# A cross-attention scan and an eight-expert layer on one core: the first conv, the hand-over to the first expert, and the order of the first copies

## The chip, the core and the metric

The kernel runs on one core of a Trainium2 chip. The metric is the device time of one execution in microseconds (us), lower is better. Engines are named as in the profile: PE is TensorE (PEld its weight loads), DVE is VectorE, ACT is ScalarE, POOL is GpSimd, SP is SyncE, which here only issues DMAs.

## The reference, cut to what matters

```python
# 1: selective scan over ctx (4 batches x 256 tokens), gated by the layer norm of x
x_in = einsum('ed,bld->bel', in_proj_w, ctx)              # 128 -> 256 channels
xc   = depthwise causal conv over time, 4 taps            # conv_w [256, 4]
u    = silu(xc + conv_b)
x_dbl = einsum('ke,bel->bkl', x_proj_w, u)                # dt_lo 8, B 16, C 16
delta = softplus(dt_proj_w @ dt_lo + dt_proj_b)
state = state * exp(delta * A) + (delta * u) * B          # 16 states per channel, 256 steps
y     = sum_n(state * C) + D * u
x     = x + (y * silu(layernorm(x)))^T

# 2: mixture of experts: 8 experts, the best 2 per token, at most 320 tokens each
probs = softmax(layernorm(x) @ Wg); gate, idx = top_k(probs, 2)
h     = relu(rows @ w1[e])                                # 256 -> 1024
out   = h @ w2[e]                                         # 1024 -> 256
x     = x + sum over the two experts of gate * out
```

## The kernel before

The work has two halves. In the first, four batches `b` of 256 tokens go through the scan; channels lie on partitions in two chunks `c`. A batch has eight steps `p` of two states each (`g = 8 b + p`, 32 steps). ACT writes the decays to PSUM, POOL the driving products `dbu`, DVE runs the scan and the product with C, PE adds the products into `y`. Everything is ordered by hand: each engine has one instruction stream and waits on named semaphores.

**The first conv.** For batches 1 to 3 the conv runs on PE: eight f32 matmuls of `ctxs`, shifted by a tap each, with folded weights `cwb` = taps times `in_proj_w` (`conv`, L783). POOL makes all of `cwb` in one multiply (L337) when the taps, copied to every partition by a DMA that is the fourth on ACT's queue (L489), are there. Batch 0 does not wait for this: PE projects `ctxs` with the bare weights (L905), and DVE applies the taps in eight operations from PSUM (L1206, L1209) into `conv0`. ACT makes `u` of both chunks (L614), PE multiplies by `wdt` (`first_dt`, L776), and ACT begins the softplus at L521. PE meanwhile goes on with `b_cast(0)`, `project`, `b_cast(1)` (L802, L756, L802), whose last result ACT copies at L538 before it makes the first decays. `keep_clock(n)` is n matmuls of ones by ones (L753) whose result nobody reads.

**The end of batch 3.** After the last step, DVE gates and adds x, and takes the layer norm's statistics; POOL raises the variance to the power -1/2 (L436); DVE makes `nmx`, minus mean over deviation (L1422), after it has chosen the two experts (`choose`); ACT makes the normalised rows (L690) and splits them into a rounded part and a rest (L693). `add_zeros(4)` adds four matmuls of zeros to `y` (L848) after steps 2, 3, 4 and 5 of this batch.

**Experts.** Each matmul of the experts is done in three: rounded part by rounded part, and each rounded part by the other's rest (`split_mm`, L1035 to L1037). So ACT makes `w1hi`, `w2hi`, `xthi`, `hthi`, and DVE or POOL the rests `w1lo`, `w2lo`, `xtlo`, `htlo`, weights by quarters. `h` has eight parts `f`; four PSUM banks hold them, so part f waits for the `htlo` of part f-4. Expert 0 gets the last batch's rows by a matmul with 0/1 columns `takes` (L1136), the others from DRAM: POOL sends every token's row by indirect DMAs into `expert_rows` (`send`, L401), SP reads an expert's rows (`rows_in`), PE turns them (`turn_rows`). For the first expert PE runs the first chunk of w1 for f = 0 to 3 (L1073, L1078), then the second chunk in the same way, and only its last four matmuls complete the four parts. `w2` of expert 0 is loaded during batch 3; ACT splits it between the relus (L708), POOL makes all four rests (L445). POOL then fetches the result rows so far (`fetch`, L455), DVE adds the expert's gated rows in the next expert (L1462, between the `htlo` of f = 1 and f = 2), and POOL sends them back (L464).

## Time and profile before

| | |
|---|---|
| median of 3 runs | 291.98 us (291.63 to 294.25) |
| the profiled execution, its own time | 291.21 us |
| its span, first to last instruction | 289.2 us |
| busy: PE, DVE, POOL, ACT | 240.7, 223.6, 222.9, 174.9 us |
| mean granted TensorE clock | 0.934 |

The scan takes the span up to about 147 us, the experts the rest. Busy shares are means over both. The granted clock is printed as a share of full speed, 1.00 for 2.4 GHz and 0.50 for 1.2 GHz; a window's value is a mean. A f32 matmul shows as two instructions.

### The profile page before, as it was taken

The page shows a single profiled execution, that of the slowest core. Times are in us where ns is not written, and L with a number is a line of the kernel's source. Part 1 is how long each engine was busy: PE and PEld are TensorE (multiplying, and loading weights), DVE is VectorE, ACT ScalarE, POOL GpSimd, SP SyncE. Part 2 cuts the span into 40 slices and gives each one's busy share as a digit, 9 for nine tenths or more (in the row PEclk, how much of TensorE's full clock was granted, in tenths as well). Part 3 has the DMA queues.
Part 4 walks back from the last instruction along what each step waited for, and adds up shares of the span by engine and source line. Part 5 has one row for each costly group of instructions (what it writes and reads, how often), then busy time and mean ns, then how long its engine had stood idle before and what let it go on. Part 6 is the DMA issues. An engine that isn't in the chain of part 4 may idle for free.

```text
span 289.2 us, 5036 instructions
## 1 busy us (share of the span) xinstructions
PE 240.7 (83%) x1568; PEld 220.2 (76%) x1568; DVE 223.6 (77%) x371; ACT 174.9 (60%) x384; POOL 222.9 (77%) x177
## 2 busy tenths in 40 slices
PE   8957695595957396668799899999999999999990
PEld 7745484475845285557798798999999999999980
DVE  2799999799899999999966766858585757575710
ACT  2889757948996776669017736475655647374500
POOL 1779779869996999999732958878787878787761
PEclk9999979888999957589799999999999999999997
DMA  6679630063003804042041566355564655655110
GB/s 160 229 201 339 209 134 0 2 201 129 0 3 97 268 0 183 2 154 101 21 137 25 200 216 217 113 210 194 170 196 187 190 214 178 226 179 180 38 59 23
DMA packets 15073, 40.38 MB, mean 140 GB/s; under 512 B 2922, under 2 KB 9900, under 8 KB 12112
## 3 DMA queue, kind: packets, MB, share of 16 engines
q1 hardware_dynamic: 11792, 33.15, 34.1%
q0 software_dynamic: 2816, 6.32, 6.4%
q10 hardware_dynamic: 448, 0.70, 1.0%
q8 instruction: 8, 0.13, 0.2%
q14 instruction: 9, 0.07, 0.1%
HBM read 32.72 MB, written 8.49 MB: 143 GB/s over the span
## 4 chain that ended last, share of the span: by engine, by line
PE 35%; POOL 6%; DVE 4%; issue 4%; DMA 3%; ACT 1%; POOLq 0%; DVEq 0%; ACTq 0%; SPq 0%
PE ps L1035 9%; PE ps L1037 9%; PE ps L1036 9%; POOL w2lo L445 3%; DVE h L1261 2%; DMA w2raw<-in_w 2%; PE ps L1044 1%; PE ps L839 1%; POOL out L464 1%; DVE hc L1273 1%; PE ps L1051 1%; DMA so_far<-out,dst 1%; PE ps L1073 1%; POOL so_far L455 1%; PE ps L753 1%
## 5 line engine op out<-in xcount | busy, mean ns | idle before, releaser
L356 POOL TENSOR_TENSOR dbu<-du,bsb 128x1024 f32<-128x1024 f32 x31 | 73.7, 2396 | 1.8 <-DMA bsb<-b_rows 0.8
L552 ACT ACTIVATE ps<-delta,anegs 128x255 f32<-128x255 f32 x128 | 53.0, 461 | 12.6 <-DVE h L1254 9.3
L1451 DVE SCALAR_TENSOR_TENSOR htlo<-ps,hthi 128x320 fp32r<-128x320 f32 x64 | 30.8, 488 | 33.6 <-ACT hthi L717 33.6
L817 PE MATMUL ps<-stack,sels 64*128 64x256 f32 x64 | 17.0, 352 | 36.8 <-DVE hc L1273 33.6
L817 PEld LDWEIGHTS ps<-stack,sels 64*128 64x128 f32 x64 | 10.8, 210 | 44.4 <-issue 44.0
L445 POOL TENSOR_TENSOR w2lo<-w2raw,w2hi 128x512 fp32r<-128x512 f32 x30 | 39.1, 1330 | 6.3 <-ACT w2hi L708 6.2
L455 POOL DMA_INDIRECT so_far<-out,dst x24 | 33.3, 1386 | 11.6 <-issue 4.7
L839 PE MATMUL ps<-cst,hc 128*128 128x128 f32 x256 | 41.7, 317 | 0.0
L1254 DVE TENSOR_TENSOR_SCAN h<-ps,dbu 128x1024 f32<-128x1024 f32 x18 | 41.1, 2283 | 0.5 <-issue 0.3
L1035 PE MATMUL ps<-xthi,w1hi 128*128 (+1 forms) x120 | 37.8, 315 | 1.2 <-DVE htlo L1451 1.2
L717 ACT ACTIVATE hthi<-ps 128x320 fp32r<-128x320 f32 x64 | 27.7, 438 | 17.1 <-PE ps L1037 15.3
L1273 DVE TENSOR_TENSOR hc<-h,ps 128x1024 f32<-128x1024 f32 x31 | 37.1, 1197 | 0.8 <-DVE h L1254 0.8
L1037 PE MATMUL ps<-xthi,w1lo 128*128 (+1 forms) x120 | 37.1, 309 | 0.0
L1036 PE MATMUL ps<-xtlo,w1hi 128*128 (+1 forms) x120 | 37.1, 309 | 0.0
L839 PEld LDWEIGHTS ps<-cst,hc 128*128 128x128 f32 x256 | 33.8, 163 | 3.9 <-issue 1.1
L1035 PE MATMUL ps<-hthi,w2hi 128*128 128x320 f32 x112 | 35.3, 315 | 0.8 <-issue 0.8
L1037 PE MATMUL ps<-hthi,w2lo 128*128 128x320 f32 x112 | 34.6, 309 | 0.0
L1036 PE MATMUL ps<-htlo,w2hi 128*128 128x320 f32 x112 | 34.6, 309 | 0.0
L1261 DVE TENSOR_TENSOR_SCAN h<-ps,dbu 128x512 f32<-128x512 f32 x28 | 32.7, 1210 | 1.8 <-ACT ps L552 1.8
L464 POOL DMA_INDIRECT out<-eo,dst x24 | 23.7, 988 | 6.9 <-issue 6.9
L401 POOL DMA_INDIRECT expert_rows<-xrow,sloti x16 | 16.2, 1014 | 11.5 <-ACT xrow L701 6.6
L1035 PEld LDWEIGHTS ps<-xthi,w1hi 128*128 128x128 f32 x120 | 22.5, 188 | 1.7 <-issue 0.9
(181 smaller groups left out, 533.1 us busy)
## 6 DMA issues: line engine op xcount, KB each, us to landing
w1raw<-in_w SPq DMA_DIRECT2D x8, 1024.0 KB, 5.2
w2raw<-in_w SPq DMA_DIRECT2D x8, 1024.0 KB, 4.8
bsb<-b_rows SPq DMA_DIRECT2D x7, 1024.0 KB, 7.2
expert_rows<-fill SPq DMA_DIRECT2D x1, 2580.0 KB, 15.6
xe<-expert_rows SPq DMA_DIRECT2D x8, 258.0 KB, 5.4
out<-x SPq DMA_DIRECT2D x4, 256.0 KB, 5.3
xnat<-in_x SPq DMA_DIRECT2D x1, 768.0 KB, 7.2
xe<-expert_rows SPq DMA_DIRECT2D x8, 64.5 KB, 5.5
```

The lines of the kernel that those rows point to most:

```text
L356: nc.gpsimd.tensor_tensor(dbu[j % DRING][:], du[:, :, None, cols(b)].to_broadcast([P, EC, 2, L]), bsb[b % 2][:, None, 2 * p:2 * p + 2, :]. ...
L445: nc.gpsimd.tensor_tensor(w2lo[:, fs, :], w2raw[:, fs, :], w2hi[:, fs, :].bitcast(F32), ALU.subtract).then_inc(s["w2lo_done"], 1)
L455: nc.gpsimd.indirect_dma_start(so_far[0:EROWS[t], t, :], None, out, bass.IndirectOffsetOnAxis(ap=dst[0:EROWS[t], e * ET + t, :], axis=0), ...
L552: ins = nc.scalar.activation(decays(g % SLOTS_DA)[:, c, i * L + 1:(i + 1) * L], delta[:, c, b * L + 1:(b + 1) * L], ACT.Exp, scale=anegs[: ...
L839: ins = nc.tensor.matmul(y[:, t, c * P:(c + 1) * P], hc[g % SUMS][:, c, i, t * P:(t + 1) * P], ident, start=False, stop=(g % PAIRS == PAIR ...
L1035: nc.tensor.matmul(out_, hi_a, hi_b, start=start, stop=False)
L1036: nc.tensor.matmul(out_, hi_a, lo_b, start=False, stop=False)
L1037: return nc.tensor.matmul(out_, lo_a, hi_b, start=False, stop=stop)
L1254: nc.vector.tensor_tensor_scan(h[g % HRING][:].rearrange("p c n t -> p (c n t)"), decays(g % SLOTS_DA).rearrange("p c t -> p (c t)"), dbu[ ...
L1261: nc.vector.tensor_tensor_scan(h[g % HRING][:, c].rearrange("p n t -> p (n t)"), decays(g % SLOTS_DA)[:, c, :], dbu[g % DRING][:, c].rearr ...
L1273: nc.vector.tensor_tensor(hc[g % SUMS][:].rearrange("p c n t -> p c (n t)"), h[g % HRING][:].rearrange("p c n t -> p c (n t)"), ps[:, c_ba ...
L1451: nc.vector.scalar_tensor_tensor(out=htlo[:, f, :], in0=ps[:, f % 4, 0:CAP], scalar=0.0, in1=hthi[:, f, :].bitcast(F32), op0=ALU.max, op1= ...
```

## The change

- **Start.** The taps' copy becomes ACT's first DMA, `in_proj_w` SP's first, ctx of batch 0 second, the small dt weights third; the first rows of x move behind `sel`. DVE makes the folded weights, one chunk at a time (two operations on 512 elements); POOL no longer does. PE runs batch 0's conv with them in two sets of four matmuls (`first_conv`) around the small `dts` product, after ten `keep_clock` matmuls in place of six; two more come behind, where six were. DVE's eight tap operations and PE's two projections are gone. The negation of `anegs` goes from DVE to POOL; on ACT the exp that feeds it and the copy of `sels` go behind the first softplus pieces.
- **End of batch 3.** `add_zeros` after steps 2 to 5 is 4, 4, 6, 2 in place of 4, 4, 4, 4. `nmx` is made by POOL from a negated mean that DVE makes before `choose`. Two `keep_clock` matmuls ahead of the last `logits` are gone.
- **First expert.** ACT splits expert 0's w2 after steps 5 and 6 of batch 3. Its first two rests are made by DVE between the first `htlo`, the last two by POOL. The second chunk of w1 runs part by part, so that part 0 is complete after three matmuls. POOL sends all first copies of the last batch's rows before the second ones; ACT writes the gates before both second copies. `turn_rows(1)` runs after f = 5 of the output in place of f = 4.

PE at the start of the program, before:

```order
L753 MATMUL ps<-onesf 128x128 x6
L905 MATMUL ps<-ctxs,inps 128x256 x2
L753 MATMUL ps<-onesf 128x128 x2
L910 MATMUL ps<-dts 128x256 x2
L753 MATMUL ps<-onesf 128x128 x6
L776 MATMUL ps<-u,wdt 128x256 x4
```

and in the changed kernel:

```order
L771 MATMUL ps<-onesf 128x128 x10
L922 MATMUL ps<-ctxs,cwb 128x256
L922 MATMUL ps<-ctxs,cwb 128x255
L922 MATMUL ps<-ctxs,cwb 128x254
L922 MATMUL ps<-ctxs,cwb 128x253
L931 MATMUL ps<-dts 128x256 x2
L922 MATMUL ps<-ctxs,cwb 128x256
L922 MATMUL ps<-ctxs,cwb 128x255
L922 MATMUL ps<-ctxs,cwb 128x254
L922 MATMUL ps<-ctxs,cwb 128x253
L771 MATMUL ps<-onesf 128x128 x2
L794 MATMUL ps<-u,wdt 128x256 x4
```

Two projections have become eight conv matmuls, and the second four stand behind the `dts` product and ahead of `first_dt`.

DVE at the start of the first expert (`xtlo` and `htlo` are rests of its rows and of h), before:

```order
L1504 TENSOR_TENSOR xtlo<-ps,xthi 128x320 x2
L1370 TENSOR_TENSOR w1lo<-w1raw,w1hi 128x2x256 x2
L1451 SCALAR_TENSOR_TENSOR htlo<-ps,hthi 128x320 x8
L1370 TENSOR_TENSOR w1lo<-w1raw,w1hi 128x2x256 x2
L1438 COPY gates<-xe 128x2
```

and in the changed kernel:

```order
L1520 TENSOR_TENSOR xtlo<-ps,xthi 128x320 x2
L1384 TENSOR_TENSOR w1lo<-w1raw,w1hi 128x2x256 x2
L1470 SCALAR_TENSOR_TENSOR htlo<-ps,hthi 128x320
L1445 TENSOR_TENSOR w2lo<-w2raw,w2hi 128x512
L1470 SCALAR_TENSOR_TENSOR htlo<-ps,hthi 128x320
L1445 TENSOR_TENSOR w2lo<-w2raw,w2hi 128x512
L1470 SCALAR_TENSOR_TENSOR htlo<-ps,hthi 128x320 x6
```

Two rests of w2 stand between the first three `htlo`.

ACT from the last batch's weights (`etop`) to the first relu (`xrow<-etop` are the gates, `xrow<-x` the second copies of the rows), before:

```order
L587 ACTIVATE etop<-top,ntop,rx 128x8 x2
L735 ACTIVATE xthi<-ps 128x320 x2
L701 ACTIVATE xrow<-x,nmx,rx 128x256
L596 ACTIVATE xrow<-etop,rsum 128x2 x2
L701 ACTIVATE xrow<-x,nmx,rx 128x256
L717 ACTIVATE hthi<-ps 128x320
L708 ACTIVATE w2hi<-w2raw 128x512
```

and in the changed kernel:

```order
L602 ACTIVATE etop<-top,ntop,rx 128x8 x2
L753 ACTIVATE xthi<-ps 128x320 x2
L611 ACTIVATE xrow<-etop,rsum 128x2 x2
L725 ACTIVATE xrow<-x,nmx,rx 128x256 x2
L735 ACTIVATE hthi<-ps 128x320 x8
L620 ACTIVATE w1hi<-w1raw 128x2x256 x2
```

The gates stand ahead of both second copies, and no split of w2 stands between the eight relus any more.

The diff, cut:

```diff
+            sp.dma_start(inps[:], inproj_t).then_inc(s["inp_in"], 16)
             sp.dma_start(ctxs[:, cols(0)], ctx_t[:, cols(0)]).then_inc(s["ctx_in0"], 16)
+            sp.dma_start(dts[:], dt_small).then_inc(s["dts_in"], 16)
             sp.dma_start(xps[:], xproj_t).then_inc(s["xps_in"], 16)
+            sp.dma_start(brow[0:XPC, 0:BC], sel).then_inc(s["sel_in"], 16)
             sp.dma_start(xnat[:, tiles_of(0), :], x[:, tiles_of(0), :]).then_inc(s["x_in0"], 16)
-            sp.dma_start(brow[0:XPC, 0:BC], sel).then_inc(s["sel_in"], 16)
...
-            pool.wait_ge(s["inp_in"], 16)
-            pool.wait_ge(s["cw_in"], 16)
-            nc.gpsimd.tensor_tensor(cwb[:], cwb[:], inps[:, None, :].to_broadcast([P, TAPS, DI]), ALU.mult
-                                    ).then_inc(s["cw_done"], 1)
+            z_rstd(1, tiles_of(0))
+            pool.wait_ge(s["a_exp"], 1)
+            nc.gpsimd.tensor_scalar(anegs[:], anegs[:], -1.0, None, ALU.mult).then_inc(s["a_neg"], 1)
             pool.wait_ge(s["small_in"], 32)
...
+            pool.wait_ge(s["ln_rstd"], B)
+            pool.wait_ge(s["mean_neg"], 1)
+            nc.gpsimd.tensor_tensor(nmx[:, tiles_of(B - 1)], pmx[:], rx[:, tiles_of(B - 1)], ALU.mult
+                                    ).then_inc(s["ln_scale"], 1)
             pool.wait_ge(s["xe_in"], 32)
-            for j in tiles_range(B - 1):
-                send(j)
+            pool.wait_ge(s["gates_done"], B)
+            pool.wait_ge(s["slots_done"], B)
+            for k in range(TOPK):
+                for t in range(BT):
+                    j = (B - 1) * BT + t
+                    if k:
+                        pool.wait_ge(s["xn_done"], j + 1)
+                    else:
+                        pool.wait_ge(s["row_done"], t + 1)
+                    nc.gpsimd.indirect_dma_start(
+                        xe_dram, bass.IndirectOffsetOnAxis(ap=sloti[:, j, k:k + 1], axis=0),
+                        xrow[:, j, k, :], None, bounds_check=SLOTS - 1, oob_is_err=False
+                    ).then_inc(s["scattered1"], 16)
...
+                if e == 0:
+                    pool.wait_ge(s["w2lo_done"], WP // 2)
+                for m in range(0 if e else WP // 2, WP // 2 if e == NE - 1 else WP):
...
-            act.dma_start(inps[:], inproj_t).then_inc(s["inp_in"], 16)
+            act.dma_start(cwb[:], conv_w[None, :, :].to_broadcast([P, TAPS, DI])).then_inc(s["cw_in"], 16)
             act.dma_start(ch[:], chan).then_inc(s["ch_in"], 16)
-            act.dma_start(dts[:], dt_small).then_inc(s["dts_in"], 16)
-            act.dma_start(cwb[:], conv_w[None, :, :].to_broadcast([P, TAPS, DI])).then_inc(s["cw_in"], 16)
             nc.scalar.preload_act_table(ACT.Silu)
...
-                act.wait_ge(s["cv_done"], c + 1)
-                nc.scalar.activation(u[:, c, cols(0)], conv0[:, c, :], ACT.Silu, bias=ch[:, c, CB:CB + 1]
+                act.wait_ge(s["conv0_psum"], c + 1)
+                nc.scalar.activation(u[:, c, cols(0)], ps[:, (CBANK, BBANK)[c], 0:L], ACT.Silu, bias=ch[:, c, CB:CB + 1]
                                      ).then_inc(s["u_done"], 1)
             nc.scalar.preload_act_table_set(EXP_SET)
+            decay_exps(0, V0BANK)
             nc.scalar.activation(anegs[:], ch[:, :, ALOG:ALOG + DS], ACT.Exp).then_inc(s["a_exp"], 1)
             act.wait_ge(s["sel_in"], 16)
             nc.scalar.activation(sels[:], brow[0:XPC, 0:BC], ACT.Copy).then_inc(s["sel_done"], 1)
-            decay_exps(0, V0BANK)
             logs(0)
...
+                if b == B - 1 and p in (5, 6):
+                    for m in range(WP // 2):
+                        split_w2(0, m + (WP // 2 if p == 6 else 0))
...
-            second_row(T // P - BT)
             weigh(B - 1)
-            second_row(T // P - 1)
+            for j in tiles_range(B - 1):
+                second_row(j)
...
+            def first_conv(c):
+                pe.wait_ge(s["cw_done"], c + 1)
+                for k in range(TAPS):
+                    ins = nc.tensor.matmul(ps[:, (CBANK, BBANK)[c], k:L], cwb[:, TAPS - 1 - k, c * P:(c + 1) * P],
+                                           ctxs[:, 0:L - k], start=(k == 0), stop=(k == TAPS - 1))
+                ins.then_inc(s["conv0_psum"], 1)
+
+            keep_clock(10, V0BANK)
             pe.wait_ge(s["ctx_in0"], 16)
-            for c, bank in ((0, WBANK), (1, CBANK)):
-                nc.tensor.matmul(ps[:, bank, 0:L], inps[:, c * P:(c + 1) * P], ctxs[:, cols(0)],
-                                 start=True, stop=True).then_inc(s["xe0_psum"], 1)
-            keep_clock(2, BBANK)
+            first_conv(0)
             pe.wait_ge(s["dts_in"], 16)
             for k in range(EC):
                 ins = nc.tensor.matmul(ps[:, YBANK, k * DI:(k + 1) * DI], dts[:, DI + k * P:DI + (k + 1) * P],
                                        dts[:, 0:DI], start=(k == 0), stop=True, skip_group_check=True)
             ins.then_inc(s["wdt_psum"], 1)
-            keep_clock(6, BBANK)
+            first_conv(1)
+            keep_clock(2, V0BANK)
...
-                    add_zeros(4)
+                    add_zeros((4, 4, 6, 2)[p - 2])
...
-            keep_clock(2, DABANK + 1)
...
-                    for c in range(KC):
+                    for c in range(KC - 1):
                         pe.wait_ge(s["xthi_done"], c + 1)
                         for f in range(4):
                             if c == 0 and f % FP == 0:
...
                         pe.wait_ge(s["xtlo_done"], c + 1)
                         for f in range(4):
                             fs = slice(f * P, (f + 1) * P)
-                            ins = nc.tensor.matmul(ps[:, f, 0:CAP], w1hi[:, c, fs], xtlo[:, c, slots],
-                                                   start=False, stop=(c == KC - 1))
-                            if c == KC - 1:
-                                ins.then_inc(s["h_psum"], 1)
+                            nc.tensor.matmul(ps[:, f, 0:CAP], w1hi[:, c, fs], xtlo[:, c, slots],
+                                             start=False, stop=(c == KC - 1))
+                    pe.wait_ge(s["xthi_done"], KC)
+                    pe.wait_ge(s["xtlo_done"], KC)
+                    for f in range(4):
+                        hidden_part(f, KC - 1).then_inc(s["h_psum"], 1)
...
-                        if first and f == 5:
+                        if first and f == 6:
...
+            dve.wait_ge(s["inp_in"], 16)
+            dve.wait_ge(s["cw_in"], 16)
+            for c in range(EC):
+                cs = slice(c * P, (c + 1) * P)
+                nc.vector.tensor_tensor(cwb[:, :, cs], cwb[:, :, cs], inps[:, None, cs].to_broadcast([P, TAPS, P]),
+                                        ALU.mult).then_inc(s["cw_done"], 1)
             dve.wait_ge(s["ch_in"], 16)
-            dve.wait_ge(s["xe0_psum"], EC)
...
+            nc.vector.tensor_scalar(pmx[:], mvx[:, tiles_of(last), 0], -1.0, None, ALU.mult).then_inc(s["mean_neg"], 1)
             choose(last)
-            dve.wait_ge(s["ln_rstd"], B)
-            nc.vector.scalar_tensor_tensor(out=nmx[:, tiles_of(last)], in0=mvx[:, tiles_of(last), 0], scalar=-1.0,
-                                           in1=rx[:, tiles_of(last)], op0=ALU.mult, op1=ALU.mult
-                                           ).then_inc(s["ln_scale"], 1)
             find_key(last)
             place(last)
             sum_weights(last)
...
+                    if first and f < WP // 2:
+                        low_w2(0, f)
```

## Rows read from the trace of the kernel before

**Rows 1.** The page: the span, and two groups of its part 5.
```profile
span 289.2 us, 5036 instructions
...
L1035 PE MATMUL ps<-xthi,w1hi 128*128 (+1 forms) x120 | 37.8, 315 | 1.2 <-DVE htlo L1451 1.2
...
L1035 PE MATMUL ps<-hthi,w2hi 128*128 128x320 f32 x112 | 35.3, 315 | 0.8 <-issue 0.8
```

**Rows 2.** Timeline, 0 to 32 us: start, duration, engine, line, operation, tiles, [idle before].
```profile
0.73 0.41 ACTq L486 DMA_DIRECT2D inps<-in_inproj_t  x1
...
6.92 1.60 PE L753 MATMUL ps<-onesf 128*128 128x128 f32 x12
...
8.79 2.35 POOL L337 TENSOR_TENSOR cwb<-cwb,inps 128x1024 f32<-128x1024 f32 x1 [7.39 <-DMA cwb<-in_conv_w]
...
8.92 1.97 PE L776 MATMUL ps<-u,wdt 128*128 128x256 f32 x8 [0.40 <-ACT u L614]
...
11.19 0.81 ACT L521 ACTIVATE w1raw<-ps,ch 128x256 f32<-128x256 f32 x2
...
13.04 0.78 DVE L1224 TENSOR_TENSOR w1raw<-w1raw 128x512 f32<-128x512 f32 x1
...
15.38 1.88 PE L783 MATMUL ps<-ctxs,cwb 128*128 128x256 f32 x8
...
15.58 0.60 ACT L538 ACTIVATE bsb<-ps 128x512 f32<-128x512 f32 x1 [1.23 <-PE ps L802]
```

**Rows 3.** DMA issues by line: KB each, median us from issue to landing.
```profile
w2raw<-in_w SPq DMA_DIRECT2D x8, 1024.0 KB, 4.8
...
cwb<-in_conv_w ACTq DMA_DIRECT2D x1, 512.0 KB, 6.4
bsb<-b_rows SPq DMA_DIRECT2D x1, 512.0 KB, 4.8
...
inps<-in_inproj_t ACTq DMA_DIRECT2D x1, 128.0 KB, 2.9
```

**Rows 4.** The chain that ended last, in order of time: start, duration, what.
```profile
143.17 1.71 PE ps L848 x8
...
157.09 1.17 PE ps L1073 x8
...
175.03 2.40 DMA so_far<-out,dst
```

**Rows 5.** Windows: busy us of PE, PEld, DVE, ACT, POOL (instructions), granted clock, DMA share, GB/s.
```profile
141.80:145.40 3.60, 3.60 (x21) 3.60 (x20) 3.60 (x5) 0.00 (x0) 2.66 (x3) 0.55 0.20 73
```

**Rows 6.** Timeline, 148 to 152 us, the end of the last batch.
```profile
148.31 0.60 ACT L562 ACTIVATE xnt<-ps 128x512 f32<-128x512 f32 x1 [6.96 <-PE ps L855]
...
149.65 0.72 POOL L436 TENSOR_TENSOR rx<-vx,nhalf 128x2 f32<-128x2 f32 x1 [2.69 <-DVE vx L1418]
...
151.17 0.15 DVE L1422 SCALAR_TENSOR_TENSOR nmx<-mvx,rx 128x2 f32<-128x2 f32 x1
...
151.36 0.60 ACT L690 ACTIVATE xrow<-x,nmx,rx 128x256 f32<-128x256 f32 x1 [2.45 <-DVE nmx L1422]
```

**Rows 7.** Timeline, 157 to 159 us, the first expert.
```profile
157.01 1.04 POOL L401 DMA_INDIRECT expert_rows<-xrow,sloti  x1 [6.65 <-ACT xrow L701]
...
158.78 0.62 ACT L708 ACTIVATE w2hi<-w2raw 128x512 fp32r<-128x512 f32 x1
...
159.55 0.39 PE L1035 MATMUL ps<-xthi,w1hi 128*128 128x320 f32 x1 [0.70 <-DVE htlo L1451]
```

**Rows 8.** Timeline of TensorE, 162 to 182 us.
```profile
164.09 0.38 PE L1035 MATMUL ps<-hthi,w2hi 128*128 128x320 f32 x1 [0.78 <-issue]
...
178.50 0.42 PE L1035 MATMUL ps<-xthi,w1hi 128*128 x1 [0.52 <-DVE htlo L1451]
```

**Rows 9.** Timeline of GpSimd, 160 to 180 us.
```profile
162.72 5.93 POOL L445 TENSOR_TENSOR w2lo<-w2raw,w2hi 128x512 fp32r<-128x512 f32 x4
172.11 1.30 POOL L455 DMA_INDIRECT so_far<-out,dst  x1 [3.46 <-DVE dst L1439]
```

52 lines of the change are left out of this document (18 added, 34 removed).

## The prediction

> **What bounds the kernel now.** I read the page first, then the waits of TensorE, then the start and the hand-over in the timeline. From the first expert on, TensorE is the bound: the 232 groups of three matmuls of the experts have only 1.2 us of idle time ahead of them in w1 and 0.8 us in w2 [rows 1]. All of it lies at three places in the first two experts: 0.70 us at 159.55, 0.78 us at 164.09, 0.52 us at 178.50 [rows 7, 8]. So behind 180 us nothing is to be won, and what is won ahead of it comes out at the end in full. In the scan the steps of DVE, ACT and POOL follow each other closely, and I take it that a shift of the first decays comes out in full too. The change touches the start, the end of batch 3, and those three places.
>
> **The start.** Call L the time at which the taps have landed. Now they land 6.4 us after an issue that is the fourth on its queue, and POOL, which waits for them and nothing else, begins at 8.79 us [rows 2, 3]. Nobody is in a hurry for them. In the changed kernel everything waits for them:
> - DVE folds the first chunk: one operation of two SBUF inputs on 512 elements takes 0.78 us [rows 2], so with the wait PE can begin at L + 0.9.
> - PE then does, without a gap, eight rows of conv, four of `dts`, eight of conv, four of `keep_clock` (two matmuls), eight of `first_dt`. Eight conv rows take 1.88 us [rows 2]. The last one's drain, some 0.16, is in that; it is the difference between the 0.31 mean of an expert's matmul [rows 1] and 0.147 of spacing (1.17 over 8 [rows 4]). So eight are 1.72, and the 28 rows of 256 columns 6.0. The four of `keep_clock` take 0.5 (1.60 over 12 [rows 2]). `first_dt` is complete at L + 0.9 + 6.0 + 0.5 + 0.2 = L + 7.6.
> - Now it is complete at 8.92 + 1.97 = 10.9 [rows 2]. PE goes on from there to `b_cast(1)`, for which ACT waits 1.23 us before the copy at 15.58 [rows 2]; the first decays follow it. So this path shifts by L + 7.6 - 10.9 = L - 3.3. The other path, ACT's softplus, starts at 11.19 [rows 2] and shifts by 0.3 less; moving `anegs` and `sels` behind it helps only there. I take L - 3.3.
>
> What is L? The issue is at 0.73, like that of `inps` now [rows 2]. From rows: 128 KB on that queue land in 2.9 us, 1024 KB from DRAM in 4.8; in between by bytes, 512 KB are 3.7, and L is 4.4. The other end is the copy most like it, also 512 KB, also one source row to all partitions, which takes 4.8 [rows 3]: L is 5.5. Some 340 KB of SP's copies go out beside it. With nothing big ahead I take the lower end and a little for company, **L = 4.6, the start 1.3 us later**; the ends are 0.9 (L = 4.2) and 2.2. It would be free only at L = 3.3, quicker than the 128 KB landed. POOL loses a multiply of 2.35 us and DVE its eight tap operations, but nobody waits for either behind this. The copies of x and the constants, moved one or two issues back, have waits only behind 11 us; nothing for them.
>
> The Trainium skill ("DMA: Bandwidth & Descriptors", "Anatomy of one DMA") gives a copy some 2.0 us fixed plus its bytes at 436 GB/s, which is 3.2 us for the taps, an L of 3.9 and a start only 0.6 us later. The trace's 4.8 us for 512 KB speaks against it, its 4.8 for 1024 KB nearly for it (4.4).
>
> **The end of batch 3.** Around 142 to 145 us the granted clock is 0.55 on average, which is 1.2 GHz for most of it [rows 5], and the four `add_zeros` of step 5 then stand in the chain with 1.71 us [rows 4], ahead of the last two steps' products. Two less save 0.86 there, but they would run into the half-speed stretch 0.6 us deeper (a row takes 1.71 / 8 = 0.21 there, half of that at full speed), and the very last products wait for DVE. I take **0.3 us earlier**; 0 if the drop of the clock moves along, 0.8 if the two more zeros at step 4 keep it away. The splits of w2, four of 0.62, fall into ACT's idle 6.96 us ahead of 148.31 [rows 6, 7], at no cost; they would cost 2.5 if that idle were not there.
>
> `nmx` now comes from DVE at 151.17, behind `choose`, and ACT's rows follow at 151.36 [rows 6]. On POOL it follows the power, which begins at 149.65 and takes 0.72 [rows 6], at about 150.45, and takes some 0.2, so it ends by 150.75. ACT's chain of rows, roundings and weights behind it is busy without a gap until `xthi`, so it moves by **0.6 us**, if PE keeps up: the two `keep_clock` fewer give `logits` 0.3, and DVE has 0.15 less ahead of `takes`. The lower end is 0.3, where `takes` decides.
>
> **The first expert.** In issue times the three gaps are larger than shown by the drain of 0.16: 0.9, 0.9 and 0.7 us. Taken with PE's first matmul of the expert as the zero: the first goes, since part 0 of h is complete after 15 matmuls and not 21, 6 x 0.147 = 0.9 earlier. The two rests of w2 that DVE now makes between the `htlo` (0.7 each by the 0.78 above) leave parts 5 and 6 late by some 0.1 each. The second goes: PE waited there for POOL's first `w2lo`, begun at 162.72 [rows 8, 9], and DVE has it by 160. The output then begins at 155.1 (where the expert's first matmul stands now: 157.09 [rows 4], behind 12 of 0.147, less 0.2) + 48 x 0.147 + 0.2 = 162.3, and the last two quarters are needed 24 matmuls later, from 165.8. POOL starts its sends when the gates are there; now it starts at 157.01 [rows 7], and with the gates one second copy earlier (0.6 [rows 6]) at about 156.5. From 157.01 to 162.72 its four sends and the memset of `so_far` take 5.7 [rows 7, 9], so it comes to w2 at 162.2, and two quarters of 5.93 / 4 = 1.5 end at 165.2; no wait. That makes 1.6 up to the second expert. But the third gap is not of w2. There DVE's `htlo` of part 2 stands behind the gated rows of the first expert, and these behind the last of POOL's three fetches (175.03 plus 2.40 [rows 4]), begun at 172.11 behind the slot numbers [rows 9]. These hang on `xthi` of expert 1, thus on `turn_rows(1)`, thus on the rows' landing and PE's place: f = 6 is reached at 162.3 + 36 x 0.147 = 167.6, against 164.09 + 30 x 0.147 = 168.5 for f = 5 now. So the fetches come only 1.1 earlier, not 1.6, and the third gap grows by the rest. **Middle: 1.1 us earlier**; ends 0.7 (rows land late) and 1.9 (fetches keep pace).
>
> **Sum.** 1.3 - 0.3 - 0.6 - 1.1 = -0.7 us. The profiled execution took 291.21, so 290.5; the median is 291.98, so 291.3. The profiled one is a little below the three runs shown. I take the middle, **290.9 us**. My own range for this case is 289.9 to 292.0.
>
> **Rivals.**
> - *The taps land early* (L = 3.9, which is also the result of the Trainium skill's rule above; or the shift is swallowed in batch 0, where POOL and DVE have slack I did not see). Start +0.5 or less: 290.1 down to 289.5. For it: no copy of weight is ahead. Against: 4.8 us for its likeness. 0.17.
> - *The hand-over gives all of it*: the fetches follow PE (1.9) and the clock does not drop (0.8). 1.3 - 0.8 - 0.6 - 1.9 = -2.0: 289.6. For it: POOL has nothing else between 165 and its fetches. Against: the order xthi, numbers, fetch. 0.15.
> - *The taps come late, and it is slower than before*: all 16 DMA engines' time goes to SP's copies issued in the same microseconds, as now, when they take 6.4 us. The start loses L - 3.3, the rest gives 2.0, so from L = 5.3 on it is slower. With 6.4 us, L is 7.1 and the time 290.9 + 2.5 = 293.4; at 4.8 us, the likeness, 291.8. 0.13.
> - *A half-speed stretch moves into 145 to 156 us*, since PE does less there (two `keep_clock` and two zeros fewer): 3.4 us at half speed cost 1.7. 292.6. 0.07.
> - *It does not do what it says*: if POOL's last two quarters came behind 165.8, PE would wait as now; then the second gap stays, 291.8. In the forecast's range, with no chance of its own.
>
> **How the numbers follow.** Forecast 0.48, rivals 0.17, 0.15, 0.13, 0.07. The range leaves out the far halves of the early and full cases and the end of the late one: 289.1 to 292.9. A measurement of this kernel can tell about 1% from no change. 1% under 291.98 is 289.06, which needs the early taps and the full hand-over together: 0.09. 1% over is 294.9, taps at 8.6 or a longer clock drop: 0.04. Within: 0.87.
>
> **What will show it.** The taps' issue to landing (3.9 forecast); the end of `first_dt` (12.2); the first decays 1.3 later than now. The power and `nmx` next to each other on POOL at 150 to 151 plus the shift. PE without idle at the first relu and the first `hthi` by `w2hi`, with a gap of more than 0.5 left in expert 1 at part 6, its releaser `htlo`, behind DVE's wait for `so_far`. What would make it wrong: a start that is no later, for then my L or my path from `first_dt` to the decays is wrong; or a gap at w2's third quarter.

## The result and the profile of the changed kernel

The changed kernel takes 293.72 us (median of 20 runs, 291.76 to 298.44), the kernel before, on the same chip, 291.73 us (20 runs, 290.84 to 294.25). The ratio is 1.0045 (95% interval 1.0024 to 1.0066), that is 1.3 us slower. The ratios here and below leave disturbed runs out, two of the 20 of the changed kernel and three of the six of rest_numbers_first among them, so that 1.3 us is less than the 2.0 between the medians. The forecast was 290.9 us and faster by 0.7; the profiled executions, 293.71 against 291.21, are 2.5 apart on the other side.

The page of the changed kernel, against [rows 1]:

```profile
span 291.9 us, 5038 instructions
...
L1055 PE MATMUL ps<-xthi,w1hi 128*128 (+1 forms) x124 | 39.3, 317 | 2.1 <-DVE htlo L1470 1.8
...
L1055 PE MATMUL ps<-hthi,w2hi 128*128 128x320 f32 x112 | 35.2, 314 | 0.0
```

The span grew by 2.7 us. The idle time in w2 is gone as forecast, but w1 has 2.1 us of it where it had 1.2, and 1.8 wait for `htlo`. Now the start, against [rows 2], in the timeline of the changed kernel:

```profile
0.99 4.64 PE L771 MATMUL ps<-onesf 128*128 128x128 f32 x20 [0.99 <-POOL onesf L318]
...
4.92 1.29 DVE L1226 TENSOR_TENSOR cwb<-cwb,inps 128x512 f32<-128x512 f32 x2 [3.66 <-DMA cwb<-in_conv_w]
...
5.73 1.96 PEld L922 LDWEIGHTS ps<-ctxs,cwb 128*128 128x128 f32 x8 [0.40 <-DMA ctxs<-in_ctx_t]
5.76 2.33 PE L922 MATMUL ps<-ctxs,cwb 128*128 128x256 f32 x8
...
8.01 1.13 PE L931 MATMUL ps<-dts 8*128 8x256 f32 x4
...
9.07 1.98 PE L922 MATMUL ps<-ctxs,cwb 128*128 128x256 f32 x8
...
10.89 0.61 PE L771 MATMUL ps<-onesf 128*128 128x128 f32 x4
...
11.34 1.89 PE L794 MATMUL ps<-u,wdt 128*128 128x256 f32 x8
...
18.42 3.25 ACT L567 ACTIVATE ps<-delta,anegs 128x255 f32<-128x255 f32 x8
```

`first_dt` ends at 13.23, before at 10.89: 2.34 us later. The first decays begin at 18.42, before at 16.08 (the first row of the next fence): 2.34 too. The DMA issues, against [rows 3], show when the data came:

```profile
cwb<-in_conv_w ACTq DMA_DIRECT2D x1, 512.0 KB, 4.1
...
inps<-in_inproj_t SPq DMA_DIRECT2D x1, 128.0 KB, 3.5
ctxs<-in_ctx_t SPq DMA_DIRECT2D x1, 128.0 KB, 4.2
```

The taps need 4.1 us from issue to landing in place of 6.4. The 128 KB of ctx beside them, issued at 1.18, need 4.2. The row of the weight loads puts their wait of 0.40 us down to ctx, but ctx was there at 1.18 + 4.2 = 5.4. The first chunk's fold, 0.69 us from 4.92, ended at 5.61 and came last.

For the stages behind, four rows of the timeline of the kernel before that the groups ahead of the prediction do not have: the first decays, the last gate product, the first matmul of the first expert, and the third expert's w1 load.

```profile
16.08 1.66 ACT L552 ACTIVATE ps<-delta,anegs 128x255 f32<-128x255 f32 x4
...
146.87 0.69 DVE L1288 TENSOR_TENSOR zst<-ps,zst 128x512 f32<-128x512 f32 x1 [1.45 <-PE ps L839]
...
155.09 0.39 PE L1073 MATMUL ps<-xthi,w1hi 128*128 128x320 f32 x1
...
176.25 0.34 SPq L285 DMA_DIRECT2D w1raw<-in_w  x1
```

The end of batch 3 in the changed kernel, against [rows 6]:

```profile
149.66 0.69 DVE L1302 TENSOR_TENSOR zst<-ps,zst 128x512 f32<-128x512 f32 x1 [0.94 <-PE ps L857]
...
152.44 0.72 POOL L436 TENSOR_TENSOR rx<-vx,nhalf 128x2 f32<-128x2 f32 x1 [2.16 <-DVE vx L1432]
...
153.24 0.20 POOL L440 TENSOR_TENSOR nmx<-pmx,rx 128x2 f32<-128x2 f32 x1
...
153.47 0.60 ACT L714 ACTIVATE xrow<-x,nmx,rx 128x256 f32<-128x256 f32 x1 [1.77 <-POOL nmx L440]
...
154.97 0.85 PE L1035 MATMUL ps<-cst,xe 128*128 128x128 f32 x6 [0.31 <-DMA xe<-expert_rows]
...
157.42 0.39 PE L1093 MATMUL ps<-xthi,w1hi 128*128 128x320 f32 x1
```

`nmx` stands behind the power as forecast. ACT's first row begins 3.81 us behind the gate product, before 4.49 (151.36 less 146.87): 0.68 won. But the first matmul of the expert wins only 0.46 (7.76 behind the gate product, before 8.22), since TensorE now waits for the rows of expert 0 from DRAM. And the first expert, against [rows 7 to 9]:

```profile
158.16 1.28 DVE L1384 TENSOR_TENSOR w1lo<-w1raw,w1hi 128x512 fp32r<-128x512 f32 x2
158.86 1.51 POOL L452 DMA_INDIRECT expert_rows<-xrow,sloti  x1 [5.43 <-ACT xrow L611]
...
160.67 0.97 POOL L452 DMA_INDIRECT expert_rows<-xrow,sloti  x1 [0.30 <-issue]
160.78 0.68 DVE L1445 TENSOR_TENSOR w2lo<-w2raw,w2hi 128x512 fp32r<-128x512 f32 x1
...
161.78 0.68 DVE L1445 TENSOR_TENSOR w2lo<-w2raw,w2hi 128x512 fp32r<-128x512 f32 x1
161.95 1.36 POOL L452 DMA_INDIRECT expert_rows<-xrow,sloti  x1 [0.30 <-issue]
...
173.13 0.41 PE L1055 MATMUL ps<-xthi,w1hi 128*128 x1 [0.29 <-ACT w1hi L620]
...
173.80 1.30 POOL L470 DMA_INDIRECT so_far<-out,dst  x1 [5.39 <-DVE dst L1458]
...
176.72 0.95 POOL L470 DMA_INDIRECT so_far<-out,dst  x1 [0.31 <-issue]
...
177.61 0.35 SPq L287 DMA_DIRECT2D w1raw<-in_w  x1
...
180.23 0.48 DVE L1481 SCALAR_TENSOR_TENSOR eo<-ps,gates,so_far 64x256 f32<-64x256 f32 x1 [1.35 <-DMA so_far<-out,dst]
...
181.16 0.41 PE L1055 MATMUL ps<-xthi,w1hi 128*128 x1 [1.82 <-DVE htlo L1470]
```

The first two gaps are gone, and the third is 1.82 us where it was 0.52. It stands behind the last `eo`, which stands behind the third fetch. That one was issued 1.69 us later than before (176.72 against 175.03 [rows 4]) but is waited for until 180.23; in the kernel before the same `eo` began at 177.57. A gap of 0.29 us is new: at 173.13 the second expert's first matmul waits for ACT's `w1hi`, which stands behind `xthi`.

Step by step, in the profiled executions:

| step | forecast | measured | from |
|---|---|---|---|
| first decays | +1.3 | +2.34 | 18.42 against 16.08 |
| the scan, to the last gate product | 0 | +0.45 | 149.66 against 146.87, less 2.34 |
| end of batch 3 | -0.9 | -0.46 | 7.76 against 8.22 |
| first expert to behind the third gap | -1.1 | +0.33 | 181.16 against 178.50, less 2.33 |
| sum | -0.7 | +2.66 | |

### The profile page after: what moved, and what is told of

It reads as the page before. It is cut to its first block, busy times and chain, and to the rows that moved or that the text cites. A ratio compares the mean times of both kernels' runs of the same rounds, so it can differ in the third digit from the quotient of the medians.

```text
span 291.9 us, 5038 instructions
## 1 busy us (share of the span) xinstructions
PE 252.0 (86%) x1572; PEld 228.0 (78%) x1572; DVE 222.1 (76%) x366; ACT 175.4 (60%) x384; POOL 220.0 (75%) x176
## 4 chain that ended last, share of the span: by engine, by line
PE 40%; DVE 7%; issue 6%; POOL 4%; DMA 4%; ACT 1%; POOLq 0%; SPq 0%; DVEq 0%; ACTq 0%
PE ps L1055 11%; PE ps L1057 10%; PE ps L1056 10%; DVE hc L1287 2%; PE ps L857 2%; DVE h L1268 2%; PE ps L1064 2%; DVE h L1275 1%; DMA so_far<-out,dst 1%; POOL out L479 1%; PE ps L1071 1%; POOL so_far L470 1%; PE ps L835 1%; DMA xe<-expert_rows 1%; DMA expert_rows<-xrow,sloti 1%
## 5 line engine op out<-in xcount | busy, mean ns | idle before, releaser
L356 POOL TENSOR_TENSOR dbu<-du,bsb 128x1024 f32<-128x1024 f32 x31 | 72.7, 2364 | 1.4 <-DMA bsb<-b_rows 1.1
L857 PE MATMUL ps<-cst,hc 128*128 128x128 f32 x256 | 44.9, 332 | 1.0 <-DVE hc L1287 1.0
L835 PE MATMUL ps<-stack,sels 64*128 64x256 f32 x64 | 18.6, 380 | 27.2 <-DVE hc L1287 24.2
L1055 PE MATMUL ps<-xthi,w1hi 128*128 (+1 forms) x124 | 39.3, 317 | 2.1 <-DVE htlo L1470 1.8
L460 POOL TENSOR_TENSOR w2lo<-w2raw,w2hi 128x512 fp32r<-128x512 f32 x28 | 36.2, 1320 | 6.4 <-ACT w2hi L627 6.2
L857 PEld LDWEIGHTS ps<-cst,hc 128*128 128x128 f32 x256 | 36.3, 171 | 5.5 <-issue 2.2
L835 PEld LDWEIGHTS ps<-stack,sels 64*128 64x128 f32 x64 | 11.8, 230 | 36.0 <-issue 36.0
L1057 PE MATMUL ps<-xthi,w1lo 128*128 (+1 forms) x124 | 38.3, 309 | 0.0
L1056 PE MATMUL ps<-xtlo,w1hi 128*128 (+1 forms) x124 | 38.3, 309 | 0.0
L1056 PEld LDWEIGHTS ps<-xtlo,w1hi 128*128 128x128 f32 x124 | 23.3, 188 | 0.0
```

Of the source, the lines that this page charges most:

```text
L356: nc.gpsimd.tensor_tensor(dbu[j % DRING][:], du[:, :, None, cols(b)].to_broadcast([P, EC, 2, L]), bsb[b % 2][:, None, 2 * p:2 * p + 2, :]. ...
L460: nc.gpsimd.tensor_tensor(w2lo[:, fs, :], w2raw[:, fs, :], w2hi[:, fs, :].bitcast(F32), ALU.subtract).then_inc(s["w2lo_done"], 1)
L835: ins = nc.tensor.matmul(ps[:, c_bank(g), i * L:(i + 1) * L], sels[:, n:n + 1].to_broadcast([XPC, P]), stack[:, cols(b)], start=(i == 0), ...
L857: ins = nc.tensor.matmul(y[:, t, c * P:(c + 1) * P], hc[g % SUMS][:, c, i, t * P:(t + 1) * P], ident, start=False, stop=(g % PAIRS == PAIR ...
L1055: nc.tensor.matmul(out_, hi_a, hi_b, start=start, stop=False)
L1056: nc.tensor.matmul(out_, hi_a, lo_b, start=False, stop=False)
```

## The experiments

Two theories stood at first. *The start* (theory A): the later start is the loss, and the rest of the change is worth about nothing. *The hand-over* (theory B): the start costs what was forecast, and the loss lies in the hand-over, where the third gap eats more than the other two gave. Eleven kernels ran in three groups of four, four and three, each against the kernel before on the same chip; its medians there were 293.3, 292.7 and 293.2 us. The traces show one execution of each. In the tables, "distance" is from the last gate product to the expert's first matmul.

**start_only.** The kernel before with the diff's first part: the DMAs' order, the folded weights on DVE, `first_conv`, ten and two `keep_clock`.

```diff
 (kernel before)
+            keep_clock(10, V0BANK)
...
+            first_conv(0)
...
+            first_conv(1)
+            keep_clock(2, V0BANK)
```

> The kernel before with the start of the change alone (order of the first copies, folded weights by DVE, first conv on TensorE, anegs on GpSimd). Theory A, the start is where the time is lost: the first decays stand at 18.4 us as in the changed kernel (16.1 before), and it is 2.0 to 2.8 us slower than before. Rival B, the loss is made later, by the expert part or by half-speed stretches that only the two halves together cause: 0.5 to 1.3 us slower at most, though the decays stand late.

Measured: 295.52 us (294.56 to 297.99), ratio 1.011 (1.0041 to 1.0178). The timeline of this kernel:

```profile
5.39 1.29 DVE L1204 TENSOR_TENSOR cwb<-cwb,inps 128x512 f32<-128x512 f32 x2 [4.13 <-DMA cwb<-in_conv_w]
...
11.44 1.89 PE L773 MATMUL ps<-u,wdt 128*128 128x256 f32 x8
...
18.52 3.25 ACT L549 ACTIVATE ps<-delta,anegs 128x255 f32<-128x255 f32 x8
```

The decays come 2.44 us later than before, and all three gaps of the kernel before are there (0.70, 0.79, 0.94). So the start alone makes it slower, by 3.2 us with an interval of 1.2 to 5.2; the 2.4 that the decays show lies in it. The taps landed half a microsecond later than in the changed kernel (the fold at 5.39 against 4.92), and `first_dt` ended only 0.1 later. TensorE waited 0.61 us ahead of the conv, and its first eight rows then took 1.89 us (6.23 to 8.12), where they take 2.25 in the changed kernel.

**rest_only.** The changed kernel with the start of before.

```diff
 (changed kernel)
-            keep_clock(10, V0BANK)
+            keep_clock(6, V0BANK)
...
-            first_conv(0)
+            for c, bank in ((0, WBANK), (1, CBANK)):
+                nc.tensor.matmul(ps[:, bank, 0:L], inps[:, c * P:(c + 1) * P], ctxs[:, cols(0)],
+                                 start=True, stop=True).then_inc(s["xe0_psum"], 1)
...
-            first_conv(1)
-            keep_clock(2, V0BANK)
+            keep_clock(6, BBANK)
```

> The kernel before with everything but the start: the end of batch 3 and the first expert as in the changed kernel. Theory A: the end of batch 3 gives some 0.5 us, the second expert begins another 1.0 to 1.5 us earlier, and the third gap of TensorE (0.52 before, 1.82 in the changed kernel) takes most of it back, so it is 0.2 to 0.8 us faster. My prediction's terms would make it 2.0 us faster. Rival B: as slow as before or slower.

Measured: 292.62 us, ratio 0.9992 (0.9951 to 1.0033). So the hand-over is worth nothing that shows, where 2.0 us were forecast. Together with start_only this bears out theory A: the start is the loss, and the rest gives next to nothing. (The two do not add up to the 1.3 us of the changed kernel, but the interval of start_only reaches down to 1.2.) Two things in its trace say where the gain went. Its third gap is as long as that of the changed kernel; and a half-speed stretch lies at the end of batch 3, where the windows give a granted clock of 0.65:

```profile
152.00:156.00 4.00, 4.00 (x26) 3.94 (x26) 2.85 (x14) 2.65 (x10) 0.00 (x0) 0.65 0.20 68
...
180.57 0.41 PE L1055 MATMUL ps<-xthi,w1hi 128*128 x1 [1.87 <-DVE htlo L1478]
```

The distance is 8.87 us there, more than the 8.22 of before.

**hand_only.** The first expert's part alone: `nmx` by DVE, four zeros at each step and the two `keep_clock` before `logits` as before.

```diff
 (rest_only)
-                    add_zeros((4, 4, 6, 2)[p - 2])
+                    add_zeros(4)
...
+            keep_clock(2, DABANK + 1)
             logits(B - 1)
```

> The kernel before with the first expert's edits alone (w2 split early, two of its rests on DVE, second chunk part by part, first copies sent first, the turn of the next rows one part later). Theory A: first two gaps of TensorE gone, the third 1.5 or more: within 0.4 us of before. If the turn one part later and the slower sends are what makes the third gap, it shows here too, without the end of batch 3.

Measured: 293.69 us, ratio 1.0024 (0.9986 to 1.0061). The distance is 8.22, as before, and no half-speed stretch lies behind 145 us. The third gap is 1.36 us, a little under the 1.5 expected.

**rest_numbers_first.** While expert 0 ends, DVE copies the second expert's slot numbers, makes the rests of its rows, and only then copies expert 0's numbers. Here expert 0's numbers go ahead of the rests. POOL's three fetches wait for both sets of numbers.

```diff
 (rest_only)
-                    rows_lo(e + 1)
                     if first:
                         metas(0, True)
+                    rows_lo(e + 1)
```

> As rest_only, but DVE copies the first expert's slot numbers ahead of the rest of the second expert's rows, so that they no longer wait for ScalarE's xthi, and GpSimd can fetch the result rows some 1 to 1.9 us earlier. Theory A (the fetches are what holds the second expert): the third gap shrinks to 0.5 us or less and it is 1.0 to 1.5 us faster than rest_only. Rival: the gap is set by how long the fetches take to land, not by when they start; then it gains under 0.4 us.

Measured: 291.87 us (288.38 to 293.31), ratio 0.9875 (0.9796 to 0.9954). The ratio goes by three runs, 288.38, 288.46 and 290.78 us; the trace is of another, of 293.26. In it the third gap is gone. Expert 0's numbers need nothing of the second expert's `xthi`; they waited for it only because DVE's `xtlo` stood ahead of them. They still stand behind the second expert's own numbers, which wait for its rows from DRAM. The half-speed stretch was there again (distance 8.83).

**start_dts_first.** To see whether `dts`, which hangs on no tap, can use the wait for the taps.

```diff
 (start_only)
-            first_conv(0)
             pe.wait_ge(s["dts_in"], 16)
...
+            first_conv(0)
             first_conv(1)
-            keep_clock(2, V0BANK)
```

> As start_only, but TensorE does the small dts product ahead of the first conv, while it waits for the taps, and the two keep_clock matmuls behind the second conv are left out: 4 rows of 256 and 4 of 128 columns less between the taps and first_dt. Theory A (the start is a sum: landing of the taps and of ctx, the fold, then every row that TensorE does): first_dt ends and the first decays stand 0.9 to 1.3 us earlier than in start_only (18.5), so at 17.2 to 17.6. Rival (the two copies land late and the rest is hidden): less than 0.4 us earlier.

Measured: 294.57 us (292.33 to 296.41), ratio 1.0055 (1.0008 to 1.0101). Timeline of one execution, of 296.10 us, and the window of the conv:

```profile
5.84 2.07 PE L908 MATMUL ps<-dts 8*128 8x256 f32 x4 [0.21 <-DMA dts<-in_dt_small]
7.84 6.42 PE L901 MATMUL ps<-ctxs,cwb 128*128 128x256 f32 x16
14.10 1.89 PE L773 MATMUL ps<-u,wdt 128*128 128x256 f32 x8
```

```profile
7.90:13.60 5.70, 5.70 (x15) 4.62 (x15) 1.00 (x4) 1.07 (x2) 1.40 (x4) 1.00 0.61 238
```

The decays begin at 21.18 in this execution, 2.7 us later than in start_only, where 0.9 to 1.3 earlier was expected. No data is missing. The conv rows come 0.43 us apart up to 13.1, the last ones and `first_dt` 0.215: half the pace, then the full pace. The column says 1.00 all the same. But the trace's records of the granted clock begin only at 13.38, with 1.00; where there is no record, the column prints 1.00 too. So the pace of the rows is what can be read there, and it is that of 1.2 GHz.

The start of every kernel here shows the same. In the changed kernel the rows of the ten `keep_clock` from 0.99 stand 0.213 us apart, those of the two at 10.89 only 0.11, and its first record of the clock is at 6.51. In start_only it is at 6.10, in the kernel before at 5.08. In after_numbers_first, whose start is word for word that of the changed kernel, it is at 10.20, and its decays begin at 20.54, not 18.42. So a late rise of the clock comes without thin rows first as well, and the order of `dts` is not shown to be its cause. Nor is the move shown to be bad: the runs of this kernel spread over 4 us, the traced one is among the slowest, and the ratio is lower than that of start_only, with intervals that overlap.

**rest_w1_waits.** The load of the third expert's w1 waits until the last of the three fetches of `so_far` has landed (they count from 0).

```diff
 (rest_only)
                     sp.wait_ge(s["h_psum"], FC * (e - 1) + W1_LATER)
+                    if e == 2:
+                        sp.wait_ge(s["so_far_in2"], 16)
```

> As rest_only, but SyncE issues the third expert's w1 load only when the last of the three fetches of result rows has landed. Theory (a TensorE that is earlier releases that load earlier, and its packets meet those of the third fetch): the third fetch lands 2.4 us after its issue in place of 3.4, and the third gap of TensorE is 1.0 us, not 1.87. Rival (the fetch is slow for a reason of its own): gap 1.7 or more, as before.

Measured: one run, 290.68 us. The timeline:

```profile
176.47 0.34 SPq L286 DMA_DIRECT2D w1raw<-in_w  x1
176.53 0.48 DVE L1491 SCALAR_TENSOR_TENSOR eo<-ps,gates,so_far 64x256 f32<-64x256 f32 x1 [0.46 <-DMA so_far<-out,dst]
177.46 0.41 PE L1057 MATMUL ps<-xthi,w1hi 128*128 x1 [0.90 <-DVE htlo L1480]
```

The last `eo` waits 0.46 us in place of 1.36, and the third gap is 0.90 in place of 1.87. So in this one execution half of that gap is gone with the load held back; that the load held the fetch up fits this. Without `keep_clock` before `logits` there was no half-speed stretch here, and the distance was 7.73.

**rest_pool_rests** and **rest_all_clock.** POOL makes expert 0's first two rests of w2 in the scan, in place of DVE in the expert, with the numbers first; the second kernel also has the `keep_clock` and zeros of before.

```diff
 (rest_numbers_first)
+            for m in range(WP // 2):
+                fs = slice(m * FP, (m + 1) * FP)
+                pool.wait_ge(s["w2hi_done"], m + 1)
+                nc.gpsimd.tensor_tensor(w2lo[:, fs, :], w2raw[:, fs, :], w2hi[:, fs, :].bitcast(F32),
+                                        ALU.subtract).then_inc(s["w2lo_done"], 1)
             pool.wait_ge(s["ln_eps"], B)
...
-                    if first and f < WP // 2:
-                        low_w2(0, f)
```

> As rest_numbers_first, but the first two rests of w2 are made by GpSimd in its idle time ahead of the last power, not by VectorE between the htlo. Theory (VectorE's operations with two SBUF inputs slow the indirect sends): the third send takes 0.97 us, not 1.36, the last one ends 0.4 us earlier after the expert's start, and the wait for the rows at turn_rows(1), 0.62, falls to 0.2. The power may start up to 0.3 us later. Time within 0.5 us of rest_numbers_first.

> As rest_pool_rests, with the two keep_clock matmuls ahead of the last logits back and four add_zeros after each of the steps 2 to 5. Theory (these matmuls of no use are what keeps the hand-over at full speed): no half-speed stretch between 145 and 160 us, and 1.0 to 1.5% faster than before, the best version so far. Rival (the stretches fall where they fall, by the phase of each run): a stretch at 151 to 157 us here too, and no difference to rest_pool_rests.

Measured: 292.28 us, ratio 0.998 (0.994 to 1.0019), and 292.08 us, ratio 0.9976 (0.9937 to 1.0015). Both times missed what was expected of them. The third gap is gone in both, but the distance is 10.4 and 9.8 us. The timeline of rest_all_clock shows why:

```profile
148.21 2.52 POOL L439 TENSOR_TENSOR w2lo<-w2raw,w2hi 128x512 fp32r<-128x512 f32 x2
148.32 2.97 DVE L1442 TENSOR_TENSOR x<-zst,xnat 128x512 f32<-128x512 f32 x1
...
161.91 0.98 POOL L458 DMA_INDIRECT expert_rows<-xrow,sloti  x1 [0.31 <-issue]
```

DVE's sum on the critical path takes 2.97 us in place of 0.69; POOL's two rests (subtractions) run beside it for 2.52. The last row shows a gain: with no rest of w2 on DVE, POOL's third send takes 0.98 us, not 1.36. rest_pool_rests had its half-speed stretch (152.3 to 155.7) and rest_all_clock none.

**numbers_first_clock**, **numbers_first_clock_w1** and **after_numbers_first.** The first is rest_numbers_first with the zeros and `keep_clock` of before, the second adds the wait of rest_w1_waits, the third is the changed kernel with the numbers' move alone.

```diff
 (rest_numbers_first)
-                    add_zeros((4, 4, 6, 2)[p - 2])
+                    add_zeros(4)
...
+            keep_clock(2, DABANK + 1)
             logits(B - 1)
```

> The start of before, the changed hand-over, expert 0's slot numbers copied ahead of expert 1's last rests, and the two keep_clock before the last logits back with four add_zeros after each of steps 2 to 5. If the missing matmuls of the end of batch 3 are what lets a half-speed stretch into 150 to 158 us, there is none there in this kernel, and the expert's first matmul stands 7.8 to 8.2 us behind the last gate product in place of 8.8. The third gap is gone or under 0.5 us, as without the matmuls. Together that is 2 to 4 us below before: 0.987 to 0.993. If the stretch has nothing to do with these matmuls, it shows up there again, and the distance stays at 8.8; if the gain of the kernel without them was chance of the clock, the ratio is 0.996 to 1.002.

> The same, and the third expert's w1 load waits for the second fetch of so_far. If the third fetch lands late because it meets this load, it lands within 2.5 us of its issue, and DVE's first gated row does not wait; but behind the numbers' earlier copy there is little left to win, so 0 to 0.3 us below the same kernel without the wait. If the wait makes the load late for the third expert, a gap appears at its first matmul.

> The changed kernel with one move: DVE copies expert 0's slot numbers ahead of expert 1's last two rests. If the gain of the first expert was lost because the three fetches followed these numbers, the fetches come 0.7 us earlier, the third gap falls from 1.8 to 0.9 us or less, and the time is 0.7 to 1.5 us below the changed kernel: ratio to before 0.998 to 1.002. The start's 2.3 us stay. If the third fetch's landing beside the w1 load is the whole of it, the fetch meets the load all the same and the gap stays over 1.3.

Measured: 289.42 us (288.85 to 291.58), ratio 0.9891 (0.9854 to 0.9929); 290.22 us, ratio 0.992 (0.9889 to 0.9952); 292.78 us, ratio 0.9989 (0.9955 to 1.0022). In numbers_first_clock the fetches come and land ahead of the load:

```profile
171.89 1.10 POOL L471 DMA_INDIRECT so_far<-out,dst  x1 [3.90 <-DVE dst L1467]
...
175.06 0.95 POOL L471 DMA_INDIRECT so_far<-out,dst  x1 [0.30 <-issue]
...
177.60 0.34 SPq L286 DMA_DIRECT2D w1raw<-in_w  x1
177.65 0.48 DVE L1490 SCALAR_TENSOR_TENSOR eo<-ps,gates,so_far 64x256 f32<-64x256 f32 x1 [0.45 <-DMA so_far<-out,dst]
```

Measured from the expert's first matmul, the first fetch is issued at 14.9 us in place of 16.4, and there is no third gap. The wait for the load adds nothing on top (what the expectation calls the second fetch is the third, as above). The changed kernel with this one move is level with the kernel before; its ratio is 0.0056 under that of the changed kernel, 1.6 us, about the third gap. The traces say the same: from the expert's first matmul to the end of the span it is 134.5 us in the changed kernel and 132.7 with the move, 134.8 in rest_only and 133.1 with the move (before 134.1).

| kernel | distance | third gap | granted clock 0.5 in 150 to 158 us | ratio |
|---|---|---|---|---|
| changed | 7.76 | 1.82 | no | 1.0045 |
| start_only | 8.22 | 0.94 | no | 1.011 |
| hand_only | 8.22 | 1.36 | no | 1.0024 |
| rest_only | 8.87 | 1.87 | yes | 0.9992 |
| rest_numbers_first | 8.83 | none | yes | 0.9875 |
| rest_w1_waits | 7.73 | 0.90 | no | one run |
| numbers_first_clock | 7.81 | none | no | 0.9891 |
| numbers_first_clock_w1 | 7.94 | none | no | 0.992 |
| after_numbers_first | 7.89 | none | no | 0.9989 |

## Why the prediction was wrong

**The start: the term was mis-sized, 1.3 us forecast, 2.34 measured.** The path was right: `first_dt` and the decays shift by the same 2.34. So was L within 0.2: the taps land 4.1 us behind 0.73, so L is 4.8 for a forecast of 4.6. What failed is the count of rows behind it, "28 rows of 256 columns 6.0" and 0.5 for the `keep_clock`. From the first conv row at 5.76 to the end of `first_dt` at 13.23 it is 7.47 us where 6.7 were planned, and that is 0.8 of the missing 1.0. Each up to the next row, the first eight conv rows took 2.25 in place of 1.72, the four of `dts` 1.06 in place of 0.86. start_only splits the 0.8. There the conv began at 6.23, when the clock had risen, and the same stretch took 7.10 us: 0.4 over the plan, about 0.2 at each of the two changes, from conv rows to those of `dts` and back. The other 0.36 is in the changed kernel alone, where the first rows ran at half pace up to 6.51. I had taken the spacing from a stretch at full pace, and put all of it into the rows. It is not the wait ahead of them: start_only waited longer, 0.61 us, and its rows were fast. The rise of the clock differs between executions of the same start (10.20 in after_numbers_first, with the decays at 20.54), and the changed start has more rows on the path to `first_dt` that it can slow: the decays lie at 18.4 to 20.5 us in the three kernels with it that keep its order, and at 15.6 to 16.6 in the nine with the start of before. The ctx of batch 0 was no term at all, and needed none: it landed before the fold ended. The rival of late taps has 2.2 us for the start at L = 5.5, near the 2.34, but through another mechanism: the taps were nearly on time. The Trainium skill's fit ("DMA: Bandwidth & Descriptors", "Anatomy of one DMA"), which that section gives for the DMAs that GpSimd issues, makes 3.2 us for the taps (an estimate). On ACT's queue they took 4.1 in this trace.

**The scan: "a shift of the first decays comes out in full" holds, and 0.45 us come on top.** The windows of the same 28 us in the changed kernel and then in the kernel before:

```profile
105.00:133.00 28.00, 23.44 (x105) 19.60 (x104) 27.31 (x36) 17.46 (x44) 26.02 (x18) 0.51 0.20 67
```

```profile
105.00:133.00 28.00, 21.03 (x121) 17.75 (x122) 27.18 (x43) 19.48 (x50) 26.57 (x17) 0.71 0.29 104
```

The granted clock is 0.51 there in place of 0.71. That this is luck of the execution rather than the change is likely: from the first decays to the last gate product it is 130.8 us in the kernel before and 131.2 in the changed one, and 130.2 to 133.1 in the eight kernels here that keep the start of before. It also tells how far to trust one pair of traces. In the runs of the kernel before that stand behind the experiments' ratios, a mean granted clock of 0.933 or 0.934 goes with 291.1 to 292.8 us, one of 0.890 or 0.891 with 293.4 to 295.5, and one of 0.895 or 0.896 with anything from 291.4 to 295.4. The two profiled executions have 0.934 and 0.897, so a microsecond of the 2.5 between them can be of the execution and not of the change.

**The end of batch 3: -0.46 for -0.9.** `nmx` gave its 0.6 (0.68 at ACT's first row). What I missed is who is late next: the rows of expert 0, sent at 149.31 by POOL and loaded again at 152.25, reach TensorE 0.31 us after it wants them. I had written "if PE keeps up" and looked at `takes` alone. The 0.3 for two zeros can't be told apart from the moves of the clock's stretches. The *half-speed stretch* rival did not happen in the changed kernel, but did in three kernels with its zeros and without the two `keep_clock`; in rest_only it goes with 1.1 us (8.87 against 7.76). In no kernel that kept both did it lie there, but in three without them it did not either, so the matmuls are not shown to be the cause. What the stretch costs in the time is open too: rest_numbers_first has a ratio no worse than numbers_first_clock, but its trace with the stretch is of a run that is not among the three behind the ratio.

**The first expert: +0.33 for -1.1, the step that failed.** The first two gaps went, for the reasons given: the output begins 7.4 us behind the expert's first matmul (164.85 less 157.42), before 9.0, 1.6 won. The third gap was foreseen at its place and with its releaser, but the sum "the fetches come only 1.1 earlier, and the third gap grows by the rest" gave 0.5 for its growth, and it grew by 1.3. One part of the miss is an error in my sum: f = 6 at 167.6 against 168.5 is 0.9 earlier, not the 1.1 that I wrote. The rest is in three things:
- The fetches came 0.6 earlier (16.4 us behind the first matmul, before 17.0), not 1.1. POOL's sends started 0.5 earlier, as forecast (156.5 against 157.01), but took longer, 1.51 and 1.36 us in place of 1.04 and 0.97, and the last ended 0.4 later than before. So the rows of the second expert landed late, the low end that I had named: `turn_rows(1)` begins at 170.20, where DVE's copy out of the same rows waits for their DMA until 170.18, and in rest_only and hand_only TensorE itself waits there, 0.22 and 0.27 us. rest_pool_rests and rest_all_clock show for the second of the two long sends (the third of four) that DVE's rest of w2 does this; for the first, which begins while a rest of w1 runs, it is argued from the same pattern. In rest_pool_rests these rows are loaded 9.45 us behind the first matmul, in the changed kernel 9.71 and before 9.78, so the long third send costs the load some 0.3 us.
- TensorE, 1.6 us ahead, released the third expert's w1 load 1.0 earlier (20.2 us behind the first matmul, before 21.2), 0.9 behind the third fetch, and the last `eo` begins 3.5 us after that fetch's issue, before 2.5. With the load held back (one execution) it is 2.6, and 0.97 is off the gap; with the numbers first it is 2.6 too. The load is not all of it: in start_only, with the hand-over of before and the load 1.5 us behind the fetch, it is 2.95.
- The second expert's first matmul waited 0.29 us for `w1hi`, which the sum did not have.

With the numbers ahead of `xtlo` the fetches go out 1.5 us earlier, the load comes behind them, and the whole third gap is gone; the 0.29 for `w1hi` stays. The prediction said that the numbers "hang on `xthi` of expert 1", and took for a dependence what is only DVE's order. The forecast that no gap comes at w2's third quarter held.

The sign was wrong because the two terms of the hand-over with the most working were followed up to where a wait disappears, and not to what is late next; the start's cost, on the path in full, was there undiminished.

## What to carry to other kernels

A gain ahead of a chain of small transfers is worth only what the transfers keep up with: when one engine gets ahead, list what it releases earlier (here the next weight load) and look which latency-bound fetch that load will meet. Take the duration of rows at the start of a program from rows at its start, where TensorE can still be at half pace, and count a change between kinds of rows as a cost of its own (0.2 us here). And before moving matmuls, see whether a few cheap operations can be put ahead of bulk work on the engine that a fetch waits for; in the changed kernel that one move was worth 0.6% (1.6 us).

## What the runs showed of the hardware

- A send by POOL (an indirect DMA of 128 rows) takes 0.97 or 0.98 us in the kernel before, the first of the last four 1.04. In the changed kernel the two that begin while a DVE operation with two SBUF inputs is running take 1.51 (at 158.86, beside `w1lo`) and 1.36 (at 161.95, beside `w2lo`). The one at 160.67 begins 0.1 us ahead of such an operation and takes 0.97. With no `w2lo` on DVE the 1.36 becomes 0.98. The Trainium skill ("SBUF — State Buffer", "Who interferes with whom") infers that such an operation leaves descriptor generation alone. These rows show that it does not leave the whole send alone; the send also reads its slot numbers from SBUF, and which part waits is not shown.
- The same section says that DVE with two SBUF inputs contends with a GpSimd instruction that reads SBUF. rest_all_clock agrees, with 2.97 us for a sum of 0.69.
- The rows of `keep_clock` stand 0.213 us apart at the start of the changed kernel and 0.11 at 10.89. In all kernels here TensorE began at this half pace, at 0.99 us, and the trace's first record of the granted clock, 1.00, came between 4.08 and 13.38 us. Up to there the column prints 1.00 without a record, and the pace of the rows has to be read instead.
